# Expert token lists built in two halves, attention exponentials normalised on GpSimd

## The reference, cut to what matters

```python
# attention of the second layer: 8 heads of 64 channels, keys from ctx
qk = jnp.einsum('bhdq,bhdl->bhql', qh, kh) * scale
sm = jax.nn.softmax(qk, axis=-1)
ret = gamma * jnp.einsum('bhql,bhdl->bhdq', sm, vh)
...
# mixture of experts: E = 64, K = 6, CAP = 96 tokens an expert, plus a shared expert
topk_w, topk_ids = _grouped_topk(logits, bias)
out = routed_moe(x, topk_w, topk_ids, w_gate, w_up, w_down) + shared(x)
```

## Time and profile before

| what | value |
|---|---|
| median of three runs | 1321.92 us (1321.69 to 1328.37) |
| the profiled execution's own time | 1323.55 us |
| its span | 1321.8 us |
| PE busy over the span | 1067.6 us |
| DVE busy | 768.2 us |
| ACT busy | 405.0 us |
| POOL busy | 545.6 us |
| mean granted clock of PE | 0.909 |

### The profile page before, as it was taken

The page is one execution under the profiler, slowest core; times in us unless marked ns, Lnnn a source line. Parts: engine busy times, 40 slices in busy tenths (PEclk is TensorE's granted clock), DMA queues, the critical chain, the costliest instruction groups (busy, mean ns, idle before and its releaser), DMA issues. The chain is left out here.

```text
span 1321.8 us, 14621 instructions
## 1 busy us (share of the span) xinstructions
PE 1067.6 (81%) x4642; PEld 509.5 (39%) x4660; DVE 768.2 (58%) x1185; ACT 405.0 (31%) x797; POOL 545.6 (41%) x437
## 2 busy tenths in 40 slices
PE   5777777747787787699999978995978888878992
PEld 3333333323333333344444443322443444434451
DVE  6999997327989899467676657891211121212221
ACT  4233332312233333266666643221111111111110
POOL 5656464127877777500101031333233333343442
PEclk8888888878899999889999989986898988889997
DMA  6434230011200000140000022419887878889642
GB/s 239 159 112 155 93 119 24 17 56 32 64 0 0 0 0 0 30 162 25 17 25 16 1 102 80 143 48 325 273 273 217 272 226 250 262 239 278 176 83 36
DMA packets 61438, 153.06 MB, mean 116 GB/s; under 512 B 9840, under 2 KB 9984, under 8 KB 61376
## 3 DMA queue, kind: packets, MB, share of 16 engines
q1 hardware_dynamic: 47312, 116.35, 25.5%
q0 software_dynamic: 14064, 35.92, 12.4%
HBM read 125.35 MB, written 26.89 MB: 115 GB/s over the span
## 5 line engine op out<-in xcount | busy, mean ns | idle before, releaser
L1594 POOL DMA_INDIRECT out<-ARENA,idx x64 | 91.8, 1435 | 237.1 <-DMA out<-ARENA,idx 206.9
L1702 DVE COPY ARENA<-PS 96x512 f32<-96x512 f32 x64 | 41.1, 682 | 177.9 <-PE PS L1637 177.9
L871 PE MATMUL PS<-SLAB,ARENA 128*128 128x512 bf16 x502 | 118.2, 383 | 22.3 <-DVE ARENA L796 20.7
L1052 DVE TENSOR_REDUCE ARENA<-PS 128x2 f32<-128x1024 f32 x64 | 78.3, 1224 | 67.9 <-PE PS L1105 67.8
L1034 POOL TENSOR_TENSOR X<-X,ARENA 128x512 f32<-128x512 f32 x16 | 20.2, 1263 | 195.6 <-DVE ARENA L1073 195.6
L1667 ACT ACTIVATE ARENA<-PS 96x192 f32<-96x192 f32 x64 | 20.9, 326 | 255.9 <-PE PS L1620 255.9
L1611 PE MATMUL PS<-ident,ARENA 96*128 96x96 f32 x256 | 43.2, 301 | 64.9 <-DMA ARENA<-rows,idx 64.9
L530 PE MATMUL PS<-CT,ARENA 128*128 x152 | 91.3, 756 | 3.1 <-issue 2.2
L1159 ACT ACTIVATE ARENA<-PS,ARENA 128x512 f32<-128x512 f32 x128 | 86.8, 683 | 10.5 <-DVE ARENA L1052 5.5
L1620 PE MATMUL PS<-SLAB,ARENA 128*96 128x384 f32 x240 | 83.1, 500 | 0.0
L871 PEld LDWEIGHTS PS<-SLAB,ARENA 128*128 128x128 bf16 x512 | 48.5, 99 | 83.9 <-issue 21.6
(11 more groups left out here) (236 smaller groups left out, 2036.6 us busy)
## 6 DMA issues: line engine op xcount, KB each, us to landing
SLAB<-in_L_ffn_w_gate SPq DMA_DIRECT2D x30, 384.0 KB
SLAB<-in_L_ffn_w_up SPq DMA_DIRECT2D x30, 384.0 KB
X<-in_L_ffn_w_down SPq DMA_DIRECT2D x14, 768.0 KB
SLAB<-in_L_ffn_w_down SPq DMA_DIRECT2D x10, 768.0 KB
CT<-in_L_ffn_w_gate SPq DMA_DIRECT2D x16, 384.0 KB
CT<-in_L_ffn_w_up SPq DMA_DIRECT2D x16, 384.0 KB
slot_out<-ARENA SPq DMA_DIRECT2D x19, 256.0 KB
X<-in_ctx SPq DMA_DIRECT2D x4, 1024.0 KB, 5.6
```

Source lines behind the costliest of these rows:

```text
L871: last = pe.matmul(bank(b), QT[:, par, k * P:(k + 1) * P], w[:, k, c * D:(c + 1) * D], start=(k == 0), stop=(k == KD - 1))
L1052: dve.tensor_reduce(nmax[:, s % 4, :], bank(2 * (s % 2), 2).rearrange("p (h d) -> p h d", h=2), AX.X, ALU.max, negate=True).then_inc(max_r ...
L1594: pool.indirect_dma_start(out, bass.IndirectOffsetOnAxis(ap=idx[0:CAP, e:e + 1], axis=0), ob[0:CAP, e % OR, :], None, compute_op=ALU.add). ...
```

## The change

In the attention every step's exponentials are normalised before they are transposed: DVE inverts the two sums of each step, and GpSimd multiplies the two 128x512 tiles of `prob` with them. PE transposes the step three behind the scores instead of two. The spread of the reciprocals, its copy, and the separate scaling and addition are gone; DVE adds the gated result to `X` in one instruction from PSUM (`leave`).

In the router stage the keys of the two halves of the tokens lie beside each other, so that one transpose of 128 columns gives 64 experts of the first half and 64 of the second on 128 partitions. DVE takes the 96 largest keys of each half over 1024 columns. PE brings the two lists of an expert to one partition, and DVE takes the 96 largest of these 192. The key transposes all stand in the middle of the second chunk's `shared_up`. The shared expert's result is added in `X` itself and stored from there. GpSimd's loop over the chunks is unrolled.

```diff
-                for i in range(NT):
-                    pool.wait_ge(pv_scaled, i + 1)
-                    pool.tensor_tensor(X[:, i, :], X[:, i, :], pv_sb[:, i % 2, :], ALU.add).then_inc(x_added, 1)
+                for s in range(STEPS4):
+                    pool.wait_ge(rec_ready, s + 1)
+                    for h in range(2):
+                        last = pool.tensor_tensor(prob[:, s % 4, h, :], prob[:, s % 4, h, :],
+                                                  rec[:, s % 4, h:h + 1].to_broadcast([P, D]), ALU.mult)
+                    last.then_inc(p_ready, 1)
...
-                def scaled(i):
+                def leave(i):
                     dve.wait_ge(pv_done, i + 1)
-                    dve.wait_ge(rec_out, i + 1)
-                    need(dve, x_added, i - 1)
-                    dve.tensor_tensor(pv_sb[:, i % 2, :], rec_sb[:, i % 2, :], bank(6 + i % 2), ALU.mult).then_inc(pv_scaled, 1)
+                    dve.scalar_tensor_tensor(out=X[:, i, :], in0=bank(6 + i % 2), scalar=tgate[:, 4:5], in1=X[:, i, :],
+                                             op0=ALU.mult, op1=ALU.add).then_inc(x_added, 1)
...
                 for s in range(STEPS4 + 8):
                     i, c = s // CH, s % CH
+                    if 1 <= s <= STEPS4:
+                        inverse(s - 1)
                     if s < STEPS4:
                         if c == 1 and i + 1 < NT:
                             queries(i + 1)
                         largest(s)
-                    if 2 <= s < STEPS4 + 2:
-                        pt1(s - 2)
-                    if c == 0 and 1 <= i <= NT:
-                        inverse(i - 1)
...
+                    if 3 <= s < STEPS4 + 3:
+                        pt1(s - 3)
...
                 def turn_p(s):
-                    pe.wait_ge(e_ready, s + 1)
+                    pe.wait_ge(p_ready, s + 1)
...
-                    if 2 <= s < STEPS4 + 2:
-                        turn_p(s - 2)
-                    if s >= 6:
-                        values((s - 6) // CH, (s - 6) % CH)
-                    if s % CH == 2 and s >= CH:
-                        spread_rec(s // CH - 1)
+                    if 3 <= s < STEPS4 + 3:
+                        turn_p(s - 3)
+                    if s >= 7:
+                        values((s - 7) // CH, (s - 7) % CH)
...
-                    sp.dma_start(out_v[:, i, :], accb[:, i % 2, :]).then_inc(acc_stored[i % 2], 16)
-                    if i == 3:
+                    sp.dma_start(out_v[:, i, :], X[:, i, :]).then_inc(acc_stored[(i + 4) // 8], 16)
+                    if i == 7:
+                        sp.wait_ge(acc_stored[0], 64)
                         load_pair(sp, 2)
                     if i == 13:
+                        sp.wait_ge(acc_stored[1], 128)
                         load_pair(sp, 3)
...
-                        need(pool, acc_stored[n % 2], g * 32 + (16 if n >= 2 else 0))
-                        pool.tensor_tensor(accb[:, n % 2, :], one(X, i), sh[:, n % 2, :], ALU.add).then_inc(acc_ready, 1)
...
+                        pool.tensor_tensor(X[:, i, :], X[:, i, :], sh[:, n % 2, :], ALU.add).then_inc(acc_ready, 1)
...
                 dve.wait_ge(key_out, 2)
...
+                def largest(chosen, among):
+
+                    for n in range(CAP // 8):
+                        eight = chosen[:, 8 * n:8 * n + 8]
+                        own.link(dve.max(eight, among))
+                        if n < CAP // 8 - 1:
+                            own.link(dve.match_replace(among, eight, among, 0.0))
+                    dve.engine_nop().then_inc(list_ready, 1)
+
+                largest(half_lists, keys)
                 dve.wait_ge(list_turned, 1)
+                own.link(dve.tensor_copy(both_lists, bank(3)[0:E1, 0:2 * CAP]))
+                largest(lists, both_lists)
+                dve.wait_ge(list_turned, 2)
...
-                turn_keys(0)
                 shared_down(0)
-                shared_up(1, 0)
-                turn_keys(1)
+                shared_up(1, 0, turn_keys)
                 shared_up(1, 1)
...
                 pe.wait_ge(list_ready, 1)
+                for h in range(2):
+                    last = pe.matmul(bank(3)[0:E1, h * CAP:(h + 1) * CAP], ident[:, h * E1:(h + 1) * E1], half_lists, start=True, stop=True)
+                last.then_inc(list_turned, 1)
+                pe.wait_ge(list_ready, 2)
                 pe.transpose(bank(3)[0:CAP, 0:E1], lists, ident[0:E1, 0:E1]).then_inc(list_turned, 1)
```

More of the change, by code:

```diff
@@ L1169, in pt0 @@
                                    ACT.Copy).then_inc(pt0_out, 1)
[L1171 to L1180 removed]
+                for s in range(STEPS4 + 3):
+                    if 3 <= s < STEPS4 + 3:
+                        pt0(s - 3)
                     if s < STEPS4:
@@ L1194, in build @@
             sem(n) for n in ("sgu_done", "ssil_ready", "ub_ready", "hs_ready", "sd_done", "sh_ready", "acc_ready"))
-        acc_stored = [sem(f"acc_stored{r}") for r in range(2)]
+        acc_stored = [sem(f"acc_stored{r}") for r in range(3)]
         place.close()
@@ L1273, in _ @@
                     sp.wait_ge(xn_stored[r], XN0 + 16 * NT // 8)
-                for r in range(2):
-                    sp.wait_ge(acc_stored[r], 16 * NT // 2)
+                for r in range(3):
+                    sp.wait_ge(acc_stored[r], (64, 128, 64)[r])
             @block.gpsimd
@@ L1303, in chunk @@
                         pool.wait_ge(sh_ready, i + 1)
-                        need(pool, acc_stored[n % 2], g * 32 + (16 if n >= 2 else 0))
-                        pool.tensor_tensor(accb[:, n % 2, :], one(X, i), sh[:, n % 2, :], ALU.add).then_inc(acc_ready, 1)
-                chunk(0)
-                with pool.Fori(1, GCH) as g:
+                        pool.tensor_tensor(X[:, i, :], X[:, i, :], sh[:, n % 2, :], ALU.add).then_inc(acc_ready, 1)
+                for g in range(GCH):
                     chunk(g)
@@ L1386, in _ @@
                 dve.wait_ge(key_out, 2)
-                for n in range(CAP // 8):
-                    eight = lists[:, 8 * n:8 * n + 8]
-                    own.link(dve.max(eight, keys))
-                    if n < CAP // 8 - 1:
-                        own.link(dve.match_replace(keys, eight, keys, 0.0))
-                dve.engine_nop().then_inc(list_ready, 1)
+                def largest(chosen, among):
[6 more added lines that the diff above has]
+                largest(half_lists, keys)
                 dve.wait_ge(list_turned, 1)
+                own.link(dve.tensor_copy(both_lists, bank(3)[0:E1, 0:2 * CAP]))
+                largest(lists, both_lists)
+                dve.wait_ge(list_turned, 2)
                 turned = bank(3)[0:CAP, 0:E1]
@@ L1442, in _, with shared_up @@
                 turn_logits(1)
-                def shared_up(g, m):
+                def shared_up(g, m, between=None):
                     need(pe, ssil_ready, 2 * g + m - 1)
@@ L1449, in shared_up @@
                     for n in ((0, 2), (1,))[m]:
+                        if n == 2 and between is not None:
+                            between()
                         last = hidden_product(pe, (bank(0), bank(6), bank(1)), wsgu, n,
```

84 lines of the change are left out of this document (30 added, 54 removed).

## The result

The changed kernel takes 1330.92 us (median of 13 runs, 1328.16 to 1334.3), the kernel before on the same chip 1323.35 (13 runs). The ratio is 1.0057, 95% interval 1.0040 to 1.0075: slower by a little more than the 0.5% that I had set as the bound, with that bound inside the interval. The profiled execution took 1331.99 us with a span of 1330.3 and a mean granted clock of 0.898 (before 1321.8 and 0.909).

A forecast was written before the change was run, and what follows sets the result against it. PE was taken to bound the attention and set the router stage. Span 1321.8 - 9.5 (attention) + 15.9 (router, clock lost) - 1.5 (experts) = 1326.7, or 1327 on the median's scale; own range 1322 to 1331, overall 1314 to 1335.

The forecast's parts named there:

- the likeliest case: Whole kernel: clock lost ahead of the first down products, 1327 us, own range 1322 to 1331, chance 0.42.
- Attention: Attention stage: spreads removed -14.1, last tile's path -1.3, later start +5.5, about -9.5 us (bounds -12 and -5).
- The start: Start of the attention: steps before the first values wait for the loop, +5.5 us (bounds 4.5 and 7.5).
- the tail: Last attention tile: ScalarE's scaling copy and GpSimd's addition leave its path, -1.3 us.
- The closed loop: Attention step: maximum, exponentials, reciprocal, next maximum take 2.81 to 3.0 us, below PE's 3.10.
- The port: Attention, port pair shared by DVE and GpSimd: DVE's query normalisation expected to win it, starting before GpSimd is released.
- The price of the rival: DVE-bound rival in the attention: query waits for GpSimd, 1.25 us more each, +12, so 1333 to 1339; chance 0.13.
- Merge: End of router stage: merging the half lists, wholly exposed after PE's last product, +10.7 us (bounds 10 and 12).
- Slack: End of router stage: last stores hold it past DVE's end today, the merge outlasts them, -3.0 us.
- Keys and clock: Router: clock lost in a 2.7 us gap ahead of first down products, +8.2, swallowing the keys' +2.0.
- Expert stage: Expert stage, untouched: starts later, with five pairs of weights landed; between 0 and -4, taken as -1.5 us.
- The faster rival: Router: late 2.7 us gap keeps its clock, -6.4, first gap harmless too; 1314 to 1315 us, chance 0.17.

The follow-up runs named there:

- the new attention alone: The kernel before with only the attention stage's change, router and additions as they were: 1318.95 us, ratio 0.996.
- 8 fillers: The changed kernel with eight unread identity transposes on PE just ahead of the first down products: 1328.87 us.
- 20 fillers: The changed kernel with twenty unread identity transposes on PE ahead of the first down products: 1318.09 us.
- the query moved: The changed kernel with twenty unread transposes ahead of the first down products, and the attention's query normalisation issued behind the maximum instead of ahead: 1323.28 us.
- keys late: The kernel before with only the first eight key transposes moved behind the first down product, making the wait ahead of it 2.7 us: 1333.57 us.

## Why the prediction was right, and where not

The time, 1330.9 for 1327, lies at the upper end of the likeliest case's own range (1322 to 1331), and the mechanisms are the ones named. By the prediction's own bound of 0.5% the outcome is "slower", which it gave 0.30; "within" had 0.50. On the profile's span the sum is better than its terms: leaving out the 3.7 us of the untouched stages ahead, the changed kernel took 1326.6 for 1326.7, because the attention (-1.9) and the router (-2.2) came out under their terms and the expert stage 4.0 over. That is luck. Step by step:

- **Attention**, -9.5: -11.4. The spreads and the steady steps came as worked out. The start cost 4.9 for 5.5, the tail gave 1.2 for 1.3. The steady part shrank by 15.1 for 14.1, and the sum of the terms (-9.9) had been rounded to -9.5. The closed loop was 2.80 to 2.82 us in the start, the lower end. GpSimd's product took 1.04 (1.07 in the mean, with those beside a query), the lower bound, not the upper that I chose:

```profile
L1032 POOL TENSOR_TENSOR ARENA<-ARENA 128x512 f32<-128x512 f32 x128 | 134.1, 1069 | 62.9 <-DVE ARENA L1058 62.9
```

- **The port.** DVE won it, as argued from the order of starts. The Trainium skill (SBUF — State Buffer, "SBUF: two separate sides") has whoever starts first hold the pair of ports that VectorE and GpSimd share for its whole instruction. The traces agree: the query takes 0.55 us when it starts ahead of GpSimd's two products, the first of which then takes up to 1.28 instead of 1.04, and 1.13 when it starts while they run. The price of the rival (1.25 more a query) was twice too high (0.58), and in that order it was hidden beside PE.
- **Merge**, +10.7: +10.2 (12.5 us from PE's last product to DVE's end, for 2.3). Slack, -3.0: -3.2. The lists of the halves took 29.6 us for 30, and their gain was worth nothing, as forecast, though from two sides: besides the merge's place on PE there are the last stores (argued).
- **Keys and clock**, +8.2: +8.4, from the shared expert's first product to the end of its last. Of this +6.2 are the first down products, +1.9 those behind them and +0.2 the last ones (the prediction had 6.4 and 1.8; it cites the 8.50 to the earlier trace rows, which has 15 of the 16 products at 8.07). PE's end in the stage moved by only +6.7, since the logits ahead took 1.6 less: before the change the clock had fallen in them, and here it hadn't. That term wasn't in the sum. The keys' own wait, +2.0, stayed hidden behind the slow products, as forecast. Where the clock is kept it was 3.8 us in three profiles, 1.4 in one and nothing in one, so no single figure would have fitted.
- **The step that failed in its reasoning**: "It fell to half (1.2 GHz) after the gap of 2.7 ... The new gap is as long as the one that lost the clock, so I take it as lost". The length of one wait doesn't settle it. An idle stretch of 1.7 us lost the clock in the profile of the new attention alone, and kept it in that of before and of 8 fillers. One of 2.7 ahead of the last down products lost it in the profile of before, kept it with 20 fillers, and lost it again with the query moved. Where hardly anything was idle (0.4 us left), the profile kept it every time. The forecast of the loss held, and the longer wait is enough for it (keys late: none of 12). But the attention part alone brings it too, and that the two parts share one loss wasn't in the sum. That the forecast named the right place with half of the reason is in part luck.
- **Expert stage**, -1.5: +2.5, the wrong sign. "Since the stage starts later, the five pairs of weights ... have all landed" is beside the point: it is the pair behind them (`t = 5`) whose loads are issued with the gathers and just ahead of them, and they start later as well. That these loads cost is shown by holding them back; that they explain the +2.5 isn't. The stage, from the first gather, took 414.3 to 420.2 us in profiles of kernels that leave it alone, with no order in them that I can name.
- **The faster rival**, 1314 to 1315, needed both waits harmless. With 20 fillers this is what happened, and the time was 1318: the keys' wait of 3.8 us and the fall behind it had no place in that rival. The one profiled execution with 8 fillers, where both waits were harmless and the keys not late, took 1316.0.

What stays open: why the attention part, or the query's place in it, decides about the clock 43 us (first down products) and 107 us (last ones) behind the attention's last values. Whether the clock had fallen in the logits goes with the outcome at the shorter wait, but not at the last down products. No run here separates the place of the idle stretches in time from their amount.

## What to carry to other kernels

Before pricing an edit on a median, look at the granted clock of each execution: a kernel may be a mixture, and an edit may only change the odds. Short waits of TensorE between dense products are worth filling with products that nobody reads, but to the last few tenths: filling a part of one bought 2 us at most. Then read in the trace what the next engine makes of it: here the keys' wait took back nearly all that the first filled wait had given, until they were moved as well. A list that is built faster gains nothing while the instruction that reads it stands last in another engine's queue: move the reader first, and only then ask whether the list is late.

## What the hardware did that I had not expected

- The kernel before runs at about 1322 to 1324 us with a mean granted clock of 0.907 or more, or at about 1332 to 1334 with 0.904 or less, one and the same program on one chip. That the router stage makes the difference is likely (keys late takes the time of the slower ones), not shown.
- A GpSimd product of 128x512 with a broadcast column takes 1.04 us, the addition of two full tiles 1.26. Where DVE's query ran beside it, it took up to 1.28.
- 2.40 us of transposes on PE that nobody reads, ahead of the first down products, and nothing else, gave 12.8 us, most of it not at that place: 1.2 us up to the last down products, 6.6 in them, 5.5 in the expert stage (by the profiles, which differ by 13.9 with the stages ahead).
